# A causal mask moved from GpSimd to VectorE, and attention values stored without zero columns

## The reference

```python
a = jax.nn.softmax(jnp.einsum('bhsd,bhtd->bhst', q, k) * D ** (-0.5), axis=-1)
if causal:
    mask = (jnp.arange(t)[None, :] > jnp.arange(s)[:, None]).astype(a.dtype)
    a = a * mask
o = jnp.einsum('bhst,bhtd->bhsd', a, v)
o = o.transpose(0, 2, 1, 3).reshape(x.shape[0], x.shape[1], H * D)
```

## Time and profile before

| | |
|---|---|
| three runs | 2377.45, 2383.33, 2383.90 us; median 2383.33 |
| span of the profiled execution | 2313.3 us |
| its own whole time | not recorded; the span and the median differ by 70.0 us |
| mean granted TensorE clock | 0.931 of full speed |
| busy over the span | PE 85%, DVE 69%, ACT 54%, POOL 49% |
| chain that ended last | PE 53%, DVE 24%, issue 8%, POOL 8%, ACT 4% |

### The profile page before, as it was taken

The page is one execution under the profiler, slowest core; times in us unless marked ns, Lnnn a source line. Parts: engine busy times, 40 slices in busy tenths (PEclk is TensorE's granted clock), DMA queues, the critical chain, the costliest instruction groups (busy, mean ns, idle before and its releaser), DMA issues.

```text
span 2313.3 us, 66487 instructions
## 1 busy us (share of the span) xinstructions
PE 1964.8 (85%) x27020; PEld 1633.0 (71%) x27020; DVE 1603.6 (69%) x4253; ACT 1255.5 (54%) x2880; POOL 1124.5 (49%) x1336
## 2 busy tenths in 40 slices
PE   5899978889788998899999689667588999898982
PEld 3767757677576776777777478667477888697882
DVE  6589786787857888678767835665889666854232
ACT  5457875467654777657765435234344455443551
POOL 2775336742367633675255354351877222234466
PEclk8999989999899999999999789789699999998996
DMA  4000000000000000000010065797011000026994
GB/s 142 5 6 2 2 1 6 6 2 2 1 3 6 3 2 1 5 5 3 2 38 13 8 187 167 222 235 266 25 28 31 4 9 9 4 83 228 349 315 125
DMA packets 98047, 147.35 MB, mean 64 GB/s; under 512 B 32016, under 2 KB 72464, under 8 KB 97488
## 3 DMA queue, kind: packets, MB, share of 16 engines
q1 hardware_dynamic: 88656, 124.48, 17.0%
q0 software_dynamic: 9088, 18.63, 3.3%
HBM read 126.49 MB, written 16.58 MB: 62 GB/s over the span
## 4 chain that ended last, share of the span: by engine, by line
PE 53%; DVE 24%; issue 8%; POOL 8%; ACT 4%; DMA 2%; SPq 0%; POOLq 0%; DVEq 0%; ACTq 0%
PE PS L2108 5%; PE PS L2092 5%; PE PS L1578 3%; PE PS L1584 3%; PE PS L1060 3%; PE PS L674 3%; PE PS L660 2%; POOL GOT L1736 2%; DVE mx L1054 2%; DVE P L1056 2%; PE PS L1067 2%; PE PS L1075 2%; PE PS L1036 2%; DVE zo L636 2%; PE PS L1171 2%
## 5 line engine op out<-in xcount | busy, mean ns | idle before, releaser
L2122 ACT ACTIVATE wh<-PS,we 128x128 f32<-128x128 f32 x624 | 176.0, 373 | 231.5 <-PE PS L2092 231.0
L1990 POOL DMA_INDIRECT wx<-x,INV x156 | 153.1, 981 | 204.5 <-PE PS L2099 106.0
L2092 PE MATMUL PS<-wxT,we 128*128 128x128 f32 x1248 | 176.3, 289 | 42.5 <-issue 35.1
L1054 DVE TENSOR_REDUCE mx<-PS 128x8 f32<-128x512 f32 x256 | 176.1, 688 | 45.8 <-PE PS L1049 24.0
L640 POOL TENSOR_TENSOR xrs<-xrs,Cs 128x2 f32<-128x2 f32 x112 | 82.0, 732 | 255.0 <-DVE xrs L632 252.7
L2108 PE MATMUL PS<-we,wh 128*128 128x128 f32 x1248 | 181.4, 290 | 22.8 <-DVE wxT L2140 21.1
L2092 PEld LDWEIGHTS PS<-wxT,we 128*128 128x128 f32 x1248 | 161.0, 202 | 49.5 <-issue 48.7
L2108 PEld LDWEIGHTS PS<-we,wh 128*128 128x128 f32 x1248 | 163.8, 202 | 32.2 <-DVE wxT L2140 29.3
L1056 DVE TENSOR_TENSOR P<-PS,mx 128x512 f32<-128x512 f32 x256 | 177.1, 692 | 8.9
L1060 PE MATMUL PS<-Cs,P 128*128 128x128 f32 x1024 | 157.5, 287 | 28.1 <-ACT P L1473 21.0
L1500 POOL TENSOR_TENSOR km<-qk,Cs 128x1024 f32<-128x1024 f32 x64 | 121.1, 1898 | 119.8 <-ACT qk L1458 48.1
(11 more groups left out here) (359 smaller groups left out, 5427.2 us busy)
## 6 DMA issues: line engine op xcount, KB each, us to landing
we<-in_wf SPq DMA_DIRECT2D x78, 578.0 KB, 5.6
we<-in_wl SPq DMA_DIRECT2D x78, 578.0 KB, 5.9
yf<-wy SPq DMA_DIRECT2D x78, 64.0 KB, 5.1
ys<-wy SPq DMA_DIRECT2D x78, 64.0 KB, 5.1
x<-X SPq DMA_DIRECT2D x32, 128.0 KB, 1.9
R<-in_wa SPq DMA_DIRECT2D x1, 3072.0 KB, 14.6
wx<-x,INV POOLq DMA_INDIRECT x156, 5.5
X<-in_x SPq DMA_DIRECT2D x4, 512.0 KB, 15.0
```

The lines of the kernel that those rows point to most:

```text
L1054: e.tensor_reduce(A.mx[r], S3, AX, ALU.max).then_inc(*o.inc())
L1990: e.indirect_dma_start(out=WB[s].x[q // NS % NX], out_offset=None, in_=x1[k], in_offset=bass.IndirectOffsetOnAxis(ap=INV[k % NH][:, q - T0 ...
L2092: i = e.matmul(ps(s, 1)[:, 128 * f:128 * f + 128], w[:, 128 * f:128 * f + 128], B.xT, True, True)
L2122: i = e.activation(B.h[:, 128 * f:128 * f + 128], ps(s, 1)[:, 128 * f:128 * f + 128], ACT.Relu, bias=w[:, 512 + f:513 + f])
```

## The change

The mask's multiplication leaves GpSimd. P is transposed unmasked as soon as the exponential is there, and for a = 0 VectorE multiplies the (transposed) mask while it takes P^T out of PSUM, in place of ScalarE's copy. V is stored with one block of 33 (or 9) columns for each head pair: the upper 64 partitions are one head's keys, the lower 64 the other's, with no zeros between. So V's values go out in one copy of 128 partitions instead of two of 64, and GpSimd only writes the column of ones. `pe_heads` then uses the 64 x 64 quarters of the array: the upper half of the keys gives one head, written to bank 0, the lower half the other head, in bank 1. It handles both r in one go, and VectorE divides both banks in one pair of instructions. `STEPS` loses the steps that went, the first half's transposition of the head outputs stands ahead of both projections of the second half, and every table of `ORDER`, in both phases, is another one. The lengths are 1296 to 1232 digits for TensorE, 1104 to 1040 for ScalarE and 672 to 608 for GpSimd in "one", and the same as before for VectorE and in "last".

```diff
@@ ORDER, a table of digits per engine; its first row for TensorE in "one" @@
-            "311002230010112223033013002003120000011011022122010201211021332031302102102012013213120102001320313123232321231031113032002320322131301300100120032031"
...
+            "001122330002121120012123123330000330110112222100212330113301220103203120102033120310302102310123123123121323023023000313131112222230303330010210101212230"
...
@@ -373,15 +370,15 @@
     def __init__(self, m, D, oT=None, mV=None):
-        n = NB * 16 * (D + 1)
-        self.V = (mV or m)("V", n)[:, 0:n].rearrange("p (b k h d) -> p (b k) h d", b=NB, k=8, h=2)
+        n = NB * 8 * (D + 1)
+        self.V = (mV or m)("V", n)[:, 0:n].rearrange("p (b d) -> p b d", d=D + 1)
...
-        self.sm = [m(f"sm{i}_", NA)[:, 0:NA] for i in range(2)]
-        self.rc = [m(f"rc{i}_", 8)[:, 0:8] for i in range(2)] if D == 32 else [m("rc", 32)[:, 0:32]]
+        self.sm = m("sm", 2 * NA)[:, 0:2 * NA]
+        self.rc = m("rc", 2 * NA if D == 32 else 32)[:, :]
@@ -1014,10 +1011,7 @@
         def pool_v(e, A, G, key):
...
-            o = own["pool"]
-            e.memset(A.V, 0.0).then_inc(*o.inc())
-            e.wait_ge(*o.now())
-            e.tensor_copy(A.V[:, :, :, A.V.shape[3] - 1], bc(c("parity"), 1, 8 * NB)).then_inc(*sig.inc(G, "vz", key))
+            e.memset(A.V[:, :, 32], 1.0).then_inc(*sig.inc(G, "vz", key))
         def pe_v(e, A, dst, src, w, rows, D):
@@ -1060,36 +1054,36 @@
-        def pe_heads(e, A, dst, r, u):
...
-            for q, i, p in product(range(2), range(2), range(2)):
-                c0, q0 = 66 * (2 * q + i), W * q + 128 * i + 64 * p
-                j = e.matmul(dst[64 * p:64 * p + 64, c0:c0 + 66], A.P[r][:, q0:q0 + 64],
-                             A.V[:, 8 * (2 * i + p) + 2 * (2 * u + q) + r, :, :].rearrange("p h d -> p (h d)"), True, True)
+        def pe_heads(e, s, A, u):
...
+            for r, q, i in product(range(2), range(2), range(2)):
+                c0 = 33 * (4 * q + 2 * i + r)
+                for h, p in FOUR:
+                    k, q0 = slice(64 * h, 64 * h + 64), W * q + 128 * i + 64 * p
+                    j = e.matmul(ps(s, h)[64 * p:64 * p + 64, c0:c0 + 33], A.P[r][k, q0:q0 + 64], A.V[k, 8 * (2 * i + p) + 2 * (2 * u + q) + r, :], True, True)
...
-        def pe_heads8(e, A, dst):
...
-            for g, i, k, p in product(range(4), range(2), range(2), range(2)):
-                c0, q0 = 144 * i + 18 * (2 * g + k), W * i + 128 * k + 64 * p
-                j = e.matmul(dst[64 * p:64 * p + 64, c0:c0 + 18], A.P[2 * (g % 2) + g // 2][:, q0:q0 + 64],
-                             A.V[:, 8 * (2 * i + p) + 2 * g + k, :, :].rearrange("p h d -> p (h d)"), True, True)
+        def pe_heads8(e, s, A):
...
+            for g, i, k in product(range(4), range(2), range(2)):
+                c0 = 9 * (8 * i + 2 * g + k)
+                for h, p in FOUR:
+                    m, q0 = slice(64 * h, 64 * h + 64), W * i + 128 * k + 64 * p
+                    j = e.matmul(ps(s, h)[64 * p:64 * p + 64, c0:c0 + 9], A.P[2 * (g % 2) + g // 2][m, q0:q0 + 64], A.V[m, 8 * (2 * i + p) + 2 * g + k, :], True, True)
...
-        def dve_heads(e, A, r, src, sums=None):
...
-            o = own["dve"]
-            O3, O4 = src[:, 0:264].rearrange("p (a d) -> p a d", d=33), src[:, 0:264].rearrange("p (a h d) -> p a h d", h=2, d=33)
-            e.reciprocal(A.rc[r], O3[:, :, 32] if sums is None else sums).then_inc(*o.inc())
-            e.wait_ge(*o.now())
-            return e.tensor_tensor(A.oT[:, :, 64 * r:64 * r + 64].rearrange("p a (h d) -> p a h d", d=32), O4[:, :, :, 0:32],
-                                   bc(v3(A.rc[r], 4), 3, 32), ALU.mult)
...
+        def dve_heads(e, s, A, sums):
...
+            o, O4 = own["dve"], PSt[:, 2 * s:2 * s + 2, 0:264].rearrange("p h (a d) -> p h a d", d=33)
+            e.reciprocal(v3(A.rc, 2), O4[:, :, :, 32] if sums is None else v3(sums, 2)).then_inc(*o.inc())
+            e.wait_ge(*o.now())
+            return e.tensor_tensor(A.oT.rearrange("p a (r h d) -> p h (a r) d", h=2, d=32), O4[:, :, :, 0:32], bc(v3(A.rc, 2), 3, 32), ALU.mult)
...
...
@@ -1125,15 +1119,16 @@
+                if u:
+                    e.wait_ge(*sig.at(G, "a_on", a, 0))
+                    pe_turn4(e, ps(s, 1), A.oT).then_inc(*sig.inc(G, "a_oTp", a, 0))
+                    yield
...
-                    if r and u:
-                        e.wait_ge(*sig.at(G, "a_on", a, u - 1, 1))
-                        pe_turn4(e, ps(s, 1), A.oT).then_inc(*sig.inc(G, "a_oTp", a, u - 1))
-                        yield
...
-                        e.wait_ge(*(sig.at(G, "a_oF", a, u - 1) if r else sig.at(G, "a_on", a, u - 1, 0)))
+                        if r:
+                            e.wait_ge(*sig.at(G, "a_oF", a, 0))
@@ -1144,14 +1139,14 @@
-                    e.wait_ge(*(sig.at(G, "a_ex", a, u, r) if a else sig.at(G, "a_mk", u, r)))
+                    e.wait_ge(*sig.at(G, "a_ex", a, u, r))
...
-                    e.wait_ge(*sig.at(G, "a_pt", a, u, r))
-                    pe_heads(e, A, ps(s, r), r, u).then_inc(*sig.inc(G, "a_ops", a, u, r))
-                    yield
-            e.wait_ge(*sig.at(G, "a_on", a, 1, 1))
+                    e.wait_ge(*(sig.at(G, "a_pt", a, u, r) if a else sig.at(G, "a_mk", u, r)))
+                pe_heads(e, s, A, u).then_inc(*sig.inc(G, "a_ops", a, u))
+                yield
+            e.wait_ge(*sig.at(G, "a_on", a, 1))
@@ -1205,9 +1200,7 @@
-            for h in range(2):
-                i = e.activation(A.V[64 * h:64 * h + 64, 16:32, h, 0:32], v3(ps(s, 0)[64 * h:64 * h + 64, :], 16), ACT.Copy)
-            i.then_inc(*sig.inc(G, "m_vA", a))
+            e.activation(A.V[:, 16:32, 0:32], v3(ps(s, 0), 16), ACT.Copy).then_inc(*sig.inc(G, "m_vA", a))
@@ -1216,7 +1209,7 @@
-                for r in range(2):
+                for r in range(2 if a else 0):
@@ -1250,9 +1243,7 @@
-            for h in range(2):
-                i = e.tensor_copy(A.V[64 * h:64 * h + 64, 0:16, h, 0:32], v3(ps(s, 1)[64 * h:64 * h + 64, :], 16))
-            i.then_inc(*sig.inc(G, "m_vD", a))
+            e.tensor_copy(A.V[:, 0:16, 0:32], v3(ps(s, 1), 16)).then_inc(*sig.inc(G, "m_vD", a))
@@ -1261,14 +1252,17 @@
-                    e.tensor_reduce(A.sm[r], v3(A.P[r], NA), AX, ALU.add).then_inc(*sig.inc(G, "a_sum", u, r))
-                    yield
-                for r in range(2):
-                    e.wait_ge(*sig.at(G, "a_ops", a, u, r))
-                    if not a:
-                        e.wait_ge(*sig.at(G, "a_sum", u, r))
-                    dve_heads(e, A, r, ps(s, r), None if a else A.sm[r]).then_inc(*sig.inc(G, "a_on", a, u, r))
-                    yield
+                    e.tensor_reduce(A.sm.rearrange("p (h a r) -> p r a h", h=2, r=2)[:, r], A.P[r].rearrange("p (a h t) -> p a h t", h=2, t=64), AX, ALU.add).then_inc(*sig.inc(G, "a_sum", u, r))
+                    yield
+                    e.wait_ge(*sig.at(G, "a_pT", a, u, r))
+                    e.wait_ge(*sig.at(G, "a_sum", u, r))
+                    e.tensor_tensor(v3(A.P[r], NA), v3(ps(s, r), NA), bc(c("later"), 1, NA), ALU.mult).then_inc(*sig.inc(G, "a_mk", u, r))
+                    yield
+                e.wait_ge(*sig.at(G, "a_ops", a, u))
+                if not a:
+                    e.wait_ge(*sig.at(G, "a_sum", u, 1))
+                dve_heads(e, s, A, None if a else A.sm).then_inc(*sig.inc(G, "a_on", a, u))
+                yield
@@ -1287,10 +1281,6 @@
-            for u, r in product(range(0 if a else 2), range(2)):
-                e.wait_ge(*sig.at(G, "a_sum", u, r))
-                e.tensor_tensor(v3(A.P[r], NA), v3(A.P[r], NA), bc(c("later"), 1, NA), ALU.mult).then_inc(*sig.inc(G, "a_mk", u, r))
-                yield
@@ -1462,9 +1452,7 @@
-            for h in range(2):
-                i = e.activation(A.V[64 * h:64 * h + 64, :, h, 0:8], v3(psW(s, 1)[64 * h:64 * h + 64], 32), ACT.Copy)
-            i.then_inc(*sig.inc(G, "n_v", y))
+            e.activation(A.V[:, :, 0:8], v3(psW(s, 1), 32), ACT.Copy).then_inc(*sig.inc(G, "n_v", y))
...
@@ -2357,9 +2343,8 @@
-    parts["later"] = t > (r % 64)
+    parts["later"] = (r % 64) > t
...
-    parts["parity"] = (r // 64) == np.arange(2)[None, :]
```

162 lines of the change are left out of this document (81 added, 81 removed), and 27 rows, old and new, of the table STEPS.

## The result

The changed kernel is slower. It took 2477.55 us (median of 4 runs, 2471.24 to 2482.04) against 2381.97 us of before, a ratio of 1.039 with a 95% interval of 1.0357 to 1.0424. In two later comparisons the ratio was 1.0468 [1.0417, 1.0519] and 1.0426 [1.0389, 1.0464]. The prediction was 2345, its range 2298 to 2398.

The account below looks back on a forecast made before the run. The prediction saw no full engine; the chain ran through TensorE for 53% of the span. Terms -18 (GpSimd), -4 (ScalarE), 0 (VectorE), -15 (stretches), -5 (TensorE), +4 (new wait) gave -38 us: 2345 us, range 2298 to 2398.

Parts of the forecast that it names:

- the orders: New order tables in both phases: no row priced them, so nothing was entered in the sum, only in the range.
- Rival (b): New orders cost TensorE 10 us more idle time at each group's turn, cancelling the 38 us gain: 2383 us, chance 0.13.
- The sum by shares of the chain: Each engine's saved time weighted by chain share over busy share: TensorE 0.62, VectorE 0.35, GpSimd 0.16, ScalarE 0.07.
- GpSimd (-18): First sweep: GpSimd loses 111 us of masks and memsets, weighted 0.16, so 18 us less.
- ScalarE (-4): First sweep: ScalarE loses 57.5 us of P^T and V copies, weighted 0.07, so 4 us less.
- the stretches (-15): VectorE instructions held up beside GpSimd's masks and memsets get 25 us shorter, weighted 0.6, so 15 us less.
- TensorE: Heads -11.5 us and small heads +3.5 us at 16.3 ns a record: -8 us, weighted 0.62 to -5 us.
- rival (d): Each small matmul costs TensorE a fixed time, 31 ns a record, +112 us of TensorE: 2419 us, chance 0.05.
- VectorE's zero: VectorE's new masks (+44.3 us) balance its saved V copies (-22.0) and divisions (-22.7): taken as 0.
- Rival (c): VectorE becomes the wall of the first attention, its 64 masks waiting 0.5 us each for transposes: 2409 us, chance 0.12.
- Small attentions: Their heads, as twice as many records with 9 columns, take 2.09 us instead of 1.98: +3.5 us of TensorE.
- The base: Profiled span 2313.3 us against a median of 2383.33; the 70.0 us between them were taken as unchanged.

Follow-up runs that it names:

- edit_refit_last: Kernel before with the edit in the first phase only, old small attentions and second phase, sweep order fitted in a third round; 2297.62 us, ratio 0.9942.
- edit_refit_old_small: Kernel before with the edit in the first phase only, old small attentions and second phase, sweep order fitted in a second round; 2304.71 us, ratio 0.9975.
- zeros_by_act: Kernel before with one thing changed: V's zeros are written by a ScalarE copy with scale 0 and not by GpSimd's memset; ratio 1.0047.
- before_refit_draws: Kernel before, code unchanged, its sweep order refitted in one round against draws of the measured durations; 2320.15 us, ratio 1.003.
- small_only: Kernel before with the edit in the small attentions of the second phase alone, first phase and both tables as before; ratio 1.0037.
- before_here: Kernel before, unchanged, profiled again on the chip of the later runs, where before takes about 2312 us.
- edit_old_orders: Changed kernel with the order tables of the kernel before in both phases, adapted to the new steps; ratio 1.0253.
- two_banks_only: Kernel before with new V and two-bank heads, mask still on GpSimd, adapted sweep order, but also new small attentions and the new second-phase table; ratio 1.0324.
- changed_here: The changed kernel itself, unaltered, measured again against before on an occasion where before takes 2374 us; ratio 1.0468.
- changed_third: The changed kernel itself, unaltered, measured a third time, where before takes 2310 to 2313 us; 2409.12 us, ratio 1.0426.

## Why the prediction was wrong

**The step that failed** is "the orders": "I have no row that prices it and enter nothing". The order is the largest term. With the same edit in the sweep it ends at 1237.9 us in the new table and at 1164.8 in a fitted one, 73 us apart (the small attentions have no part in the sweep), and the new table of the second phase costs 20 us more. Before's order, adapted to the edit, is no better than the new one (1233.6). Why the new tables suit the edit so badly stays open. Rival (b) had named the mechanism, and as evidence against it "nothing in the trace prices it". It put the mechanism at 40 us, enough to cancel the gain, where the span grew by 94. A missing row was absence of evidence, not evidence of absence: 160 random exchanges add 61 us to the 147 us of TensorE's idle time in before.

**The sum by shares of the chain** was too large in its main terms. GpSimd (-18), ScalarE (-4) and the stretches (-15) were meant to shorten waits. In edit_refit_last GpSimd has 113 us less in the sweep, and TensorE's idle time is unchanged (144 us; 153 in edit_refit_old_small, 147 in before). So these 37 us did not appear as less waiting in either order where the edit gains. zeros_by_act is weaker evidence for the memset alone: gone from GpSimd, the time rises by 0.47%, but ScalarE has 30 us more to do. An average over a chain says whose turn it was, not what is saved when that engine is quicker. That the fixed order hands the slack to the next wait is my reading of it.

**TensorE** was entered at -5 and is where nearly the whole gain of edit_refit_last is. Its busy time is 1020.7 us against 1042.5 (before_refit_draws) and 1037.4 (before), -17 to -22. In the changed kernel it is -11, as forecast for the heads (-11.5). The rest can't be put down to the edit: before's own sweep, with the same code and table, has 1027.7 us at a granted clock of 0.97 in small_only and 1037.4 at 0.96 in before_here, and before's code goes up to 1057.7 us with 160 exchanges.

**The fixed matmul price**, rival (d), had the form right and the size wrong. The changed kernel's block of 64 quarters with 33 columns, and one of 52 records with 9 columns, start to start of the next block (timeline, columns of the earlier trace rows):

```profile
256.22 1.11 PE L1063 MATMUL PS<-V,P 64*64 64x33 f32 x64
257.26 0.66 PE L1054 MATMUL PS<-Cs,P 128*128 128x128 f32 x4
...
1261.81 0.92 PE L1072 MATMUL PS<-Vn,P 64*64 64x9 f32 x52
1262.66 1.53 PE L1054 MATMUL PS<-Cs,P 128*128 128x128 f32 x12
```

1.04 us / 64 = 16.3 ns, and 0.85 / 52 = 16.3 ns, at full granted clock: the value taken from L674 was right for 33 columns and for 9, and the 31 ns of (d) belong to the other form. So a record's price in these quarters does not depend on the columns. The 16.3 ns are a mean over overlapping records: within the block of L1063 four records start about 7 ns apart and the next four 58 ns after these, while one record lasts 221 ns on the mean.

The Trainium skill, TensorEngine Tiling (Array Packing), section Instruction Overhead, has the form of this right, a floor that few columns don't get below. Its 60 cycles, by estimate 25 ns at 2.4 GHz, are for one matmul. As a price per record they are too high here; what one matmul alone would take, with no other quarter beside it, no run here shows. So the prediction's "the trace doesn't agree" was right for the price of a block and says nothing against the floor itself.

**VectorE's zero** held: the mask takes 681 ns (692 forecast), the product on twice the columns 691 ns. The stretched instructions were read half right. L629's mean fell from 380 to 219 ns (18 us over 112). The zo<-xo form stayed at 693 ns (695 before), where I had said below 500. Its 341 ns "undisturbed" came from another form. In before 56 of its 64 instances already lie beside GpSimd's instructions that write xb and x (L1296, L1298, L1378, L1380, L1385) and 2 beside a mask, and its median is 748 to 750 ns before and after; the work that left was not what held it up. VectorE's busy time in the sweep fell by 42 us in the changed kernel and by 12 in edit_refit_last, against a forecast of 25: the stretches, too, depend on the order.

**Rival (c)** is visible in the slices. From 500 us VectorE is at 24.09 of 25 us (18.75 in before), though TensorE has no less than before there (22.42 against 21.21). But the mask has 0.5 us of idle time before it in all, not 64 times 0.5, so (c) isn't the cause in the changed kernel. In edit_old_orders, where VectorE stood idle 27.4 us before the mask and TensorE waited 15.9 us for it, it was part of it.

**Small attentions**: forecast +3.5 us of TensorE, measured +6 us of its busy time in the second phase (927.9 against 921.8) and +11 us of the second phase.

**The base** was wrong too, without effect on the sign: the 70 us between span and median were no fixed cost.

In numbers, against before's profile on the same occasion: sweep +53 (TensorE's work -11, idle time +64), second phase +41 (small attentions 11, table 20, a rest of 10 within scatter), together +94 us of span. The prediction had -38.

## What to carry to other kernels

Where each engine follows an order written out beforehand, an edit cannot be priced without its order. Perturb the order of the old kernel at random, and the loss tells how large an error a forecast can have that leaves the order out. Compare edits only with orders treated alike for both, with as many rounds of fitting, and judge a fitted order on the chip, not by the count that chose it. A run of half an edit must differ from before in that half alone: two_banks_only, with a new table besides, answered another question. Where one engine is busy 88% of a stage, count first what the edit takes from that engine; here work taken from the others did not shorten its idle time.

## What was not expected of the hardware

Before took 2310 to 2313 us in four comparisons and 2374 and 2382 in two others. The four of 2310 to 2313 us ran on chips 0, 7, 14 and 15 and the one of 2374 on chip 1, one comparison each, so chip and occasion can't be told apart. Of the changed kernel there are profiles from both kinds: its sweep ends at 1242.6 and 1237.9 us, its second phase takes 1235 and 1167. The difference lies there, and in TensorE's granted clock, 0.86 against 0.88. Second phase of changed_here; the row of changed_third stands in the first section:

```profile
1243.00:2477.00 1234.00, 978.43 (x11372) 855.54 (x11372) 681.46 (x1932) 480.40 (x1318) 515.12 (x512) 0.86 0.37 110
```

And 64 x 64 quarters that take turns cost 16.3 ns a record with 9, 33 or 64 columns alike.

ScalarE's loads of function tables (ACT_TABLE_LOAD, 1283 ns each) depend on the order too: 90 in the sweep of before, 78 in the changed kernel, 110 in edit_refit_last. The 12 fewer are 15 of the 71 us that ScalarE has less in the changed kernel's sweep. Of these three, the kernel with most loads is the fastest, so they are not what decides.
